# A perceiver block on one core: the block of the four stages is closed without GpSimd's own drain

## The reference

```python
x = x + _L0_xattn_ref(_layernorm(x), ctx_1024, ctx_1024, ...)   # cross-attention with distance bias
x = x + _L0_attn_ref(_layernorm(x), ...)                        # causal attention, ratio scores
x = x + _L0_ffn_ref(_layernorm(x), ...)                         # quantised feed-forward
x = x + _L1_xattn_ref(_layernorm(x), ctx_1024, ...)             # cross-attention
x = x + _L1_attn_ref(_layernorm(x), ...)                        # long and by-segment attention, fused
x = x + _L1_ffn_ref(_layernorm(x), router_weight, w1, w2)       # 8 experts, 2 for each token

# _L1_ffn_ref
probs = softmax(x @ router_weight)
_, topk_idx = top_k(probs, 2)
local_probs = probs * one_hot(topk_idx, 8).sum(axis=1)
y1, y2 = split(einsum('th,ehf->tef', x, w1), 2)
o = einsum('tef,efh->teh', silu(y1) * y2, w2)
out = einsum('teh,te->th', o, local_probs)
```

## Time and profile before

| | us |
|---|---|
| median of three runs | 707.64 (707.36 to 707.98) |
| the profiled execution, its whole time | 707.23 |
| its span, first to last instruction | 705.4 |

### The profile page before, as it was taken

One profiled execution on the slowest core, in us unless ns is written; L12 is line 12 of the kernel. 1 busy time (PEld: TensorE's weight loads), 2 busy tenths in 40 slices (PEclk: granted clock), 3 DMA queues, 4 the chain that ended last, 5 costly groups with the idle time before them and its releaser, 6 DMA issues.

```text
span 705.4 us, 18761 instructions
## 1 busy us (share of the span) xinstructions
PE 621.6 (88%) x7075; PEld 476.0 (67%) x7075; DVE 460.2 (65%) x1279; ACT 366.2 (52%) x992; POOL 315.3 (45%) x458
## 2 busy tenths in 40 slices
PE   4999999999999999769947999989999758999990
PEld 3787888788877787534425876568888545777760
DVE  1797777777776898844888835478999873333320
ACT  1665666565656898643945634356665521222220
POOL 1346666666652898300000212075756414656641
PEclk9999999999999999969966999999999978999995
DMA  8833233333300000293001447075020032444434
GB/s 268 264 107 89 81 76 92 85 77 84 89 5 3 4 4 4 55 341 113 0 0 45 195 180 291 10 303 221 4 69 2 2 106 56 67 66 64 62 39 73
DMA packets 31704, 65.20 MB, mean 92 GB/s; under 512 B 5792, under 2 KB 21792, under 8 KB 29312
## 3 DMA queue, kind: packets, MB, share of 16 engines
q1 hardware_dynamic: 26016, 55.73, 24.0%
q0 software_dynamic: 4688, 7.18, 6.5%
q10 hardware_dynamic: 912, 1.10, 0.5%
HBM read 57.67 MB, written 7.37 MB: 92 GB/s over the span
## 4 chain that ended last, share of the span: by engine, by line
PE 64%; DVE 21%; ACT 3%; issue 3%; DMA 2%; SPq 2%; POOL 1%; DVEq 0%; ACTq 0%; POOLq 0%
PE psum L2648 8%; PE psum L491 7%; PE psum L499 7%; PE psum L2658 4%; PE psum L529 4%; PE psum L1502 3%; PE psum L1479 3%; PE psum L868 3%; DVE ff_peak L1520 2%; PE psum L515 2%; PE psum L544 2%; PE psum L859 2%; PE psum L851 2%; PE psum L899 2%; DMA wn<-in_w_down 2%
## 5 line engine op out<-in xcount | busy, mean ns | idle before, releaser
L802 POOL TENSOR_SCALAR bias<-dist,cst 128x257 f32<-128x257 f32 x128 | 61.1, 496 | 74.8 <-issue 43.0
L491 PE MATMUL psum<-ctxT,shared 128*128 128x257 f32 x256 | 65.9, 401 | 2.3 <-DMA msk<-in_mask 2.2
L424 ACT ACTIVATE prob<-s_sb,negm 128x257 f32<-128x257 f32 x128 | 64.9, 509 | 1.0 <-DVE negm L665 0.9
L499 PE MATMUL psum<-shared,ctxT 128*128 128x256 f32 x256 | 60.8, 380 | 0.0
L661 DVE CUSTOM_DVE_ANT_0 s_sb<-psum,bias 128x257 f32<-128x257 f32 x128 | 46.6, 421 | 20.0 <-PE psum L515 17.1
L1741 POOL TENSOR_TENSOR wn<-wn,cst 128x1 f32<-128x1 f32 x8 | 4.7, 588 | 122.7 <-DVE wn L1868 122.7
L2648 PE MATMUL psum<-ex_w,shared 128*128 x184 | 58.3, 460 | 0.6 <-ACT shared L2541 0.6
L491 PEld LDWEIGHTS psum<-ctxT,shared 128*128 128x128 f32 x256 | 47.1, 194 | 12.5 <-issue 4.9
L413 ACT COPY kT<-psum 128x257 f32<-128x257 f32 x64 | 24.0, 374 | 60.3 <-PE psum L491 60.3
L499 PEld LDWEIGHTS psum<-shared,ctxT 128*128 128x128 f32 x256 | 46.5, 191 | 5.1
L2648 PEld LDWEIGHTS psum<-ex_w,shared 128*128 128x128 f32 x184 | 33.1, 190 | 15.4 <-issue 0.8
(11 more groups left out here) (357 smaller groups left out, 1610.9 us busy)
## 6 DMA issues: line engine op xcount, KB each, us to landing
ctxT<-in_ctx_T SPq DMA_DIRECT2D x32, 257.0 KB
ex_w<-in_w SPq DMA_DIRECT2D x1, 5632.0 KB, 17.2
kpos<-in_kpos SPq DMA_DIRECT2D x32, 128.5 KB
msk<-in_mask SPq DMA_DIRECT2D x32, 128.5 KB
near_turned<-in_ctx_T_tiles SPq DMA_DIRECT2D x4, 1028.0 KB
ff_used_up<-in_ctx_T_tiles SPq DMA_DIRECT2D x4, 1028.0 KB
near_rows<-in_ctx_tiles SPq DMA_DIRECT2D x4, 1024.0 KB, 8.0
ff_used_up<-in_ctx_tiles SPq DMA_DIRECT2D x4, 1024.0 KB, 7.7
```

What stands on the lines that cost most here:

```text
L424: nc.scalar.activation(prob[n % 2][:, g, :], s_sb[n % 2][:, g, :], ACT.Exp, bias=negm[:, b, g:g + 1], accum_out=esum[t % 2][:, b, g:g + 1]) \
L491: ins = nc.tensor.matmul(kv[m][:, 0:SK], w["xa_k"][:, k, P * m:P * m + P], ctxT[n % BT][:, k, :], start=(k == 0), stop=(k == KT - 1))
L499: ins = nc.tensor.matmul(kv[0][:, D * i:D * i + D], ctxT[n % BT][:, k, P * i:P * i + P], w["xa_v"][:, k, :], start=(i == 0 and k == 0), st ...
L802: nc.gpsimd.tensor_scalar(bias[n % 2][:, g, :], dist[n % 2][:], c.slope[:, g:g + 1], 1.0 / FAR, ALU.mult, ALU.mult).then_inc(bias_ready, 1)
```

## The change

It is one argument, in `build`:

```diff
-        with nc.Block() as block:
+        with nc.Block(no_gpsimd_drain=True) as block:
             for stage in (attentions, ffn_and_context, segments, segments_and_experts):
                 stage(block)
         nc.clear_and_free_semaphores(own)
         nc.all_engine_barrier()
```

## The result

| | before | after |
|---|---|---|
| median, us | 707.63 (6 runs, 705.44 to 709.5) | 703.4 (6 runs, 702.29 to 703.74) |
| ratio | | 0.9937, 95% interval 0.9918 to 0.9955 |
| profiled execution, us | 707.23 | 702.29 |
| span, us | 705.4 | 700.5 |

The kernel is faster by 4.2 us in the medians, 0.6%. The forecast was 707.4 us and no change, with a range down to 705.4.

What follows compares the result with a forecast made beforehand. GpSimd's serial closing instructions were taken to bound the end. Removing L219's drain, with L222's lengthening: -3.915 - 0.167 + 3.915 = -0.17 us, taken as -0.2; median 707.64 - 0.2 = 707.4 us, range 705.4 to 708.4.

Steps and rivals of the forecast that it cites:

- What bounds the end: After the merge lands at 700.1 us, the last 5.3 us are closing instructions alone, in series on GpSimd's queue.
- The price of the removed drain: L219's GpSimd drain at the block's end: 3.915 us itself plus some 0.04 us of handing on, about 3.96 us.
- What the 3.9 us are: L219's drain: something GpSimd must finish or tidy after 47 software DMAs, done once, met by the first drain behind them.
- The length of L222's drain: Drain of the semaphore clearing, bounded by 0.167 and 3.915 us; upper end taken, leaving a gain of about 0.2 us.
- The argument that misled: Middle drains L837 and L2347, of L222's form, end 0.15 to 0.2 us behind GpSimd's last work, so this form waits.
- The second place for the bill: If L222's drain leaves the work, L223's plain drain at the last barrier takes it; the sum differs by hundredths.
- The first rival: Cost goes with L219's drain; those of L222 and L223 stay at 0.167 and 0.046 us: 703.7 us, chance 0.10.
- The slower rival: Tidying paid twice, in L222's drain and again in L223's behind the range clear: another 3.9 us, 711.3 us, chance 0.03.
- The range of the main case: Cost moved to a later closing drain: 706.7 to 708.2 us, from -0.4 to 0 change and run spread; chance 0.82.
- The added instructions: Separate semaphore raises behind the other four engines' drains: hundredths of a us each, with 12 us of cover before GpSimd asks.

## Why the prediction was wrong

- **What bounds the end**: right. The closing instructions stand in series on GpSimd's queue behind the merge, and nothing lies beside them. Branch to end went from 5.27 to 1.34 us.
- **The price of the removed drain**, 3.96 us: right. The result repeats this term: branch to end is 3.93 us shorter.
- **What the 3.9 us are**: half right. They come from the software DMAs, are owed once, and the next plain drain meets them if the first is gone. The drain behind the block's barrier and the one of the last barrier without the clearing both took 3.915 us. But they are not a rest of work that GpSimd does by itself. They are 0.0823 us for each of 47 DMAs, spent when a plain drain asks.
- **The length of L222's drain**: the step that failed. The prediction put it between 0.167 and 3.915 us and took the upper end, "since the row it is nearest to is the one at the same place behind the same DMAs". It measured 0.163 us. Place and history were the wrong measure of nearness; the form of the instruction was the right one. Behind the software DMAs the drain with a range took 0.061 to 0.173 us in every run, whether a plain drain stood before it or not. With that length in the sum, -3.915 - 0.167 + 0.163 = -3.92 us comes out in place of -0.17.
- **The argument that misled**: "the form with a semaphore range waits as well", from L837 and L2347. These rows show that it waits for compute in flight, and the kernel after repeats them (0.984 and 3.914 us). They stand before GpSimd's first DMA, so they could say nothing of DMAs. From one kind of wait I concluded on another.
- **The second place for the bill**, L223: it fell with the same step. That drain does pay in full where nothing with a range stands before it, and took 0.062 us where something does. I had not thought of a drain that cancels a debt and does not pay it.
- **The first rival** had the right time, 703.7 us, for a reason that was wrong: the cost did not go with this instruction, since a plain drain at two other places brought it back. It went because all that follows it is either of the other form or behind that form. The words against it ("both would have to find nothing to do") describe what happened.
- **The slower rival**, a second payment in L223: did not occur, 0.062 us.
- **The range of the main case**, 706.7 to 708.2 us, is wider than what it is said to be made of: 707.36 - 0.4 = 706.96 to 707.98. Nothing hangs on it.
- **The added instructions** on the other four engines cost nothing that shows; they raise the barrier at 687.1 and earlier, and GpSimd asks at 699.4.
- **The rule of the Trainium skill** (PSUM — Partial Sum Buffer, Engine vs sequencer instructions: a drain waits for the engine to go fully idle) does not tell the two forms apart. The drain with a range agrees with it: 0.061 us with no work of GpSimd in flight. For the plain drain it leaves the cost open: 3.915 us with no work in flight that the trace shows, in proportion to the DMAs and not to time.

## What to carry to other kernels

Where GpSimd has issued many DMAs, look for its plain drains on the path to the end, in the view of the single lines and not in the busy time: here each cost 0.08 us for every such DMA since the last drain, however small. Remove them only where each DMA is waited for by its own semaphore and the semaphores are cleared behind it, as here; then neither the landing nor the count is left to the drain. What the dropped work would have been for, no run here shows. And when a row is to stand for an unknown cost, take it from the same form of instruction with the same kind of work before it; the nearest place is not the nearest case.

## What the runs showed of the hardware

- A plain GpSimd drain behind software DMAs takes 0.046 us and 0.082 us for each since the last drain: 0.119 us behind one, 3.915 behind 47, 5.222 behind 63, all landed. 4.7 us of waiting and 12 memsets in between change nothing.
- A drain with a semaphore range takes 0.061 us (a range of one semaphore) or 0.163 us (the range 121 to 197) with 47 such DMAs before it and no drain between, and makes the next plain drain short (0.059 and 0.062 us). Behind compute in flight it takes 0.98 and 3.91 us, until that has ended. Whether it waits for a DMA in flight was not tried.
